# Softplus's last sum on GpSimd, residual sums as adding transfers, the router's last product in token layout, and new beats for a kernel of 16 batches

## The reference

```python
x = x + layernorm(attn(layernorm(x)))     # attn: a selective scan (Mamba block)
x = x + layernorm(ffn(layernorm(x)))      # ffn: two branches of 8 low-rank experts

# attn(x), di = 512 channels, N = 16 states, 4 taps
h = x * rsqrt(mean(x * x) + EPS) * norm_scale
xs, res = split(h @ w_in);  res = silu(res);  xs = silu(causal_conv(xs) + conv_b)
delta, B, C = split(xs @ w_xproj, [16, 32])
delta = softplus(delta @ w_dt + b_dt)
state[t] = exp(delta[t] * A) * state[t-1] + (delta[t] * xs[t]) * B[t]      # per channel and state
y[t] = sum over the 16 states of state[t] * C[t]
return x + ((y + xs * D) * res) @ w_out

# ffn(x), per branch (Q, K, V, W, U differ)
prod = (Q @ V) * cumsum(K @ W)                        # 8 experts of rank 64
weights = softmax(gelu(Q @ router_w1.T + b1) @ router_w2.T + b2 + expert_bias)   # 8 values a token
out = ((prod * weights) @ U + weights @ b) / (t + 1)
return (fwd + 0.5 * inv) @ W_O.T
```

## Time and profile before

| | |
|---|---|
| median of 3 runs | 2423.53 us (2418.75 to 2423.81) |
| the profiled execution | 2417.08 us, of which the span of instructions is 2415.1 us |
| first scan starts, last scan ends | 68.2 and 2294.9 us |
| busy: VectorE, TensorE, GpSimd, ScalarE | 2173.3, 2128.0, 1854.3, 1842.0 us |
| transfers | 101.69 MB, in mean 42 GB/s |

### The profile page before, as it was taken

One profiled execution on the slowest core, in us unless ns is written; L12 is line 12 of the kernel. 1 busy time (PEld: TensorE's weight loads), 2 busy tenths in 40 slices (PEclk: granted clock), 3 DMA queues, 4 the chain that ended last, 5 costly groups with the idle time before them and its releaser, 6 DMA issues.

```text
span 2415.1 us, 35863 instructions
## 1 busy us (share of the span) xinstructions
PE 2128.0 (88%) x9268; PEld 1287.7 (53%) x9268; DVE 2173.3 (90%) x2820; ACT 1842.0 (76%) x3897; POOL 1854.3 (77%) x1324
## 2 busy tenths in 40 slices
PE   5587789898998989899898989989898998988888
PEld 2355455464655546465554645555464655545454
DVE  1899999999999999999999999999998999999921
ACT  6575787869688786978778697887869788785644
POOL 3869797887879788787878878797887879787620
PEclk8797899999999999999999999999999999999999
DMA  6011110211102020111102021110202001011100
GB/s 139 31 40 41 31 49 19 67 31 59 36 28 58 18 71 28 62 32 34 52 20 68 28 62 33 30 55 23 67 27 62 31 29 56 21 60 34 31 2 16
DMA packets 83400, 101.69 MB, mean 42 GB/s; under 512 B 23480, under 2 KB 49872, under 8 KB 83168
## 3 DMA queue, kind: packets, MB, share of 16 engines
q1 hardware_dynamic: 83168, 99.06, 13.6%
HBM read 90.13 MB, written 8.91 MB: 41 GB/s over the span
## 4 chain that ended last, share of the span: by engine, by line
DVE 34%; issue 26%; PE 19%; POOL 11%; ACT 8%; DVEq 1%; DMA 1%; POOLq 0%; ACTq 0%; SPq 0%
DVE h L1347 15%; DVE yT L1363 11%; PE bank L798 10%; POOL bx L766 5%; PE stateT L971 3%; PE bank L950 3%; DVE xs L1257 2%; ACT decay L1217 2%; POOL scratch L684 1%; POOL scratch L690 1%; DVE rows L1283 1%; DVE prod L1329 1%; POOL dx L694 1%; PE bank L936 1%; DVE cumT L1303 1%
## 5 line engine op out<-in xcount | busy, mean ns | idle before, releaser
L766 POOL TENSOR_TENSOR bx<-dx,B_rows 128x1024 f32<-128x1024 f32 x512 | 1204.8, 2366 | 224.3 <-DVE h L1347 183.8
L1347 DVE TENSOR_TENSOR_SCAN h<-decay,bx 128x512 f32<-128x512 f32 x1024 | 1238.6, 1210 | 65.6 <-ACT decay L1217 54.8
L1217 ACT ACTIVATE decay<-delta,decay_rate 128x512 f32<-128x512 f32 x1024 | 703.2, 693 | 273.5 <-DVE h L1347 270.4
L971 PE MATMUL stateT<-ident,h 128*128 128x128 f32 x4096 | 640.7, 288 | 200.7 <-DVE h L1347 107.0
L971 PEld LDWEIGHTS stateT<-ident,h 128*128 128x128 f32 x4096 | 482.6, 146 | 541.1 <-issue 269.1
L1363 DVE SCALAR_TENSOR_TENSOR yT<-stateT,C_tok,yT 128x512 f32<-128x512 f32 x960 | 696.4, 726 | 24.9 <-PE stateT L971 23.8
L798 PE MATMUL bank<-k_to_expert,cumT 128*128 128x512 f32 x512 | 261.2, 635 | 6.8 <-DVE prod L1329 6.7
L798 PE MATMUL bank<-q_to_expert,xnT 128*128 128x512 f32 x512 | 249.2, 611 | 0.0
L798 PE MATMUL bank<-hT,w_in_sb 128*128 128x512 f32 x512 | 243.2, 600 | 5.5 <-DVE rows L1283 3.6
L1183 ACT ACTIVATE cum_sb<-bank,gate 128x64 f32<-128x64 f32 x1024 | 222.7, 328 | 28.7 <-PE bank L798 26.9
L950 PE MATMUL bank<-expert_to_out,prodT 128*128 128x256 f32 x1024 | 239.2, 379 | 0.0
(11 more groups left out here) (155 smaller groups left out, 2578.4 us busy)
## 6 DMA issues: line engine op xcount, KB each, us to landing
B_rows<-B_scratch SPq DMA_DIRECT2D x256, 256.0 KB, 3.2
x_front<-in_L_attn_x SPq DMA_DIRECT2D x16, 512.0 KB, 4.9
x_back<-in_L_attn_x SPq DMA_DIRECT2D x16, 512.0 KB, 4.1
out<-x_back SPq DMA_DIRECT2D x16, 512.0 KB, 4.2
w_in_sb<-in_L_attn_w_in SPq DMA_DIRECT2D x1, 1024.0 KB, 5.9
cum_sb<-in_L_ffn_V_fwd SPq DMA_DIRECT2D x2, 256.0 KB
prod<-in_L_ffn_W_inv_exp SPq DMA_DIRECT2D x2, 256.0 KB
xnT<-in_L_ffn_W_fwd SPq DMA_DIRECT2D x2, 256.0 KB
```

The source lines that it names most:

```text
L766: pool.tensor_tensor(bx[use % BX_RING][:, :, :], dx[q.parity][:, 2 * half:2 * half + 2, :], row, ALU.mult).then_inc(s_bx.step(f"{n},{half} ...
L971: last = pe.transpose(stateT[j % 2][:, c * P:(c + 1) * P], h[n % 2][:, c, j * P:(j + 1) * P], ident[:, :])
L1217: act.activation(decay[c % 2][:, :], delta[q.parity][:, c, :], ACT.Exp, scale=decay_rate[:, c, n:n + 1]).then_inc(s_exp.step(f"{n},{c}"), 1)
L1347: dve.tensor_tensor_scan(h[n % 2][:, c, :], decay[c % 2][:, :], bx[(2 * n + c // 2) % BX_RING][:, c % 2, :], 0.0, ALU.mult, ALU.add).then_ ...
```

## The change

Four edits in one.

1. `d1` moves from VectorE to GpSimd, with the same operation on the same tiles. All that waited for VectorE's d1 (decays, `dx`, reuse of `scratch`) waits for GpSimd's.
2. `x1` and `x` become transfers that GpSimd issues, from `rows` and `o_rows` into `x_back`, both in SBUF, with `accum_op=ALU.add`; `x` is one transfer of all 512 KB instead of two halves. `st1` and the store wait for the transfers' semaphores.
3. `logit` takes blocks of 128 tokens of `scratch` as the stationary operand and 8 columns of weights as the moving one, so that the result has tokens on partitions. ScalarE's copy and `logit_rows` fall away; TensorE has one use of a bank fewer a period. The wait for the batch before's last output product moves from the copy to `gateT`.
4. `TIMETABLE` is new throughout.

```diff
-    ("F", "sq", "act"): (12,),
+    ("F", "sq", "act"): (2,),
-    ("F", "w", "pool"): (102, 103, 119, 124),
-    ("F", "w2", "pool"): (102, 105, 122, 125),
-    ("F", "d1", "dve"): (96, 105, 123, 123),
-    ("F", "row", "sp"): (87, 110, 113),
+    ("F", "w", "pool"): (100, 107, 118, 120),
+    ("F", "w2", "pool"): (103, 111, 120, 125),
+    ("F", "d1", "pool"): (105, 113, 125, 126),
+    ("F", "row", "sp"): (111, 117, 136),
...
-    ("F", "silu", "act"): (70,),
+    ("F", "silu", "act"): (66,),
-    ("B", "rb", "pool"): (301,),
-    ("B", "t", "act"): (299,),
-    ("B", "x1", "pool"): (304,),
-    ("B", "st1", "dve"): (304,),
+    ("B", "rb", "pool"): (305,),
+    ("B", "t", "act"): (303,),
+    ("B", "x1", "pool"): (307,),
+    ("B", "st1", "dve"): (307,),
-    ("B", "xnT", "pe"): (317, 317),
-    ("B", "rt", "pe"): (324, 325, 327, 330),
+    ("B", "xnT", "pe"): (316, 318),
+    ("B", "rt", "pe"): (320, 325, 327, 330),
...
-    ("L", "out", "pe"): (373, 382, 396, 396, 434, 436, 438, 443),
+    ("L", "out", "pe"): (378, 387, 397, 398, 438, 442, 447, 451),
-    ("L", "rs", "pool"): (454,),
-    ("L", "t", "act"): (468,),
-    ("F", "dx", "pool"): (108, 109, 127, 131),
-    ("L", "x", "pool"): (476, 479),
-    ("L", "store", "sp"): (471,),
+    ("L", "rs", "pool"): (464,),
+    ("L", "t", "act"): (469,),
+    ("F", "dx", "pool"): (113, 115, 129, 130),
+    ("L", "x", "pool"): (478,),
+    ("L", "store", "sp"): (463,),
...
             def store(batch, k, use):
-                sp.wait_ge(l_pool.sem, l_pool.done(batch, "x1"))
+                sp.wait_ge(out_added, batch.count(16, 16))
...
+            def d1_task(b, c, use):
+                pool.wait_ge(f_act.sem, f_act.done(b, f"ln{c}"))
+                pool.wait_ge(f_pool.sem, f_pool.done(b, f"w2{c}"))
+                pool.tensor_tensor(delta[b.parity][:, c, :], delta[b.parity][:, c, :], scratch[:, 2 + c % 2, :], ALU.add).then_inc(f_pool.step(f"d1{c}"), 1)
...
             def x_task(b, k, use):
-                half = slice(2 * k, 2 * k + 2)
-                pool.wait_ge(l_act.sem, l_act.done(b, f"t{2 * k + 1}"))
-                pool.tensor_tensor(x_back[b.parity][:, half, :], x_back[b.parity][:, half, :], o_rows[:, half, :], ALU.add).then_inc(l_pool.step(f"x{k}"), 1)
+                pool.wait_ge(l_act.sem, l_act.done(b, "t3"))
+                pool.sem_inc(passed["pool"], 1)
+                pool.dma_start(x_back[b.parity][:, :, :], o_rows[:, :, :], accum_op=ALU.add).then_inc(out_added, 16)
...
             def x1_task(b, k, use):
                 pool.wait_ge(b_act.sem, b_act.done(b, "t3"))
-                pool.tensor_tensor(x_back[b.parity][:, :, :], x_back[b.parity][:, :, :], rows[:, :, :], ALU.add).then_inc(b_pool.step("x1"), 1)
+                pool.sem_inc(passed["pool"], 1)
+                pool.dma_start(x_back[b.parity][:, :, :], rows[:, :, :], accum_op=ALU.add).then_inc(back_added, 16)
...
-                matmuls(use.bank[0:2 * KE, :], [(w2_padded[:, m, (1 - br) * KE:(3 - br) * KE], scratch[:, 2 * br + m, :])
-                                                for br in range(2) for m in range(DT)]).then_inc(b_pe.step("lg"), 1)
+                for j in range(TB):
+                    for br in range(2):
+                        columns = slice((2 * j + br) * KE, (2 * j + br + 1) * KE)
+                        last = matmuls(use.bank[:, columns], [(scratch[:, 2 * br + m, j * P:(j + 1) * P], w2_padded[:, m, KE:2 * KE]) for m in range(DT)])
+                last.then_inc(b_pe.step("lg"), 1)
```

More of the change, by code:

```diff
@@ L144 @@
-    ("B", "logit", "act"): (343,),
-    ("B", "logit_rows", "pe"): (343,),
-    ("B", "lb", "dve"): (342,),
-    ("B", "mx", "dve"): (344,),
-    ("B", "sub", "pool"): (353,),
-    ("B", "ex", "act"): (349,),
+    ("F", "sq", "act"): (2,),
+    ("F", "rs", "pool"): (18,),
+    ("F", "h", "act"): (19,),
+    ("F", "hT", "pe"): (21, 23),
+    ("F", "hT", "act"): (23, 26),
+    ("F", "x", "sp"): (102,),
+    ("F", "xs", "pe"): (32, 34, 36, 38),
+    ("F", "xs", "act"): (35, 36, 38, 42),
+    ("F", "cvA", "dve"): (34, None, 37, None),
@@ new lines @@
+    ("F", "cvB", "dve"): (35, None, 38, None),
+    ("F", "cvC", "dve"): (36, None, 39, None),
+    ("F", "tap", "act"): (None, 38, None, 42),
+    ("F", "cv", "pool"): (None, 45, None, 60),
+    ("F", "res", "pe"): (36, 42, 45, 53),
+    ("F", "res", "act"): (41, 44, 53, 61),
+    ("F", "silu", "act"): (66,),
+    ("F", "proj", "pe"): (79,),
+    ("F", "proj", "act"): (84,),
+    ("F", "B", "sp"): (86,),
+    ("F", "Ct", "pe"): (117,),
+    ("F", "Ct", "act"): (122,),
+    ("F", "dt", "pe"): (85, 87, 93, 103),
@@ new lines @@
+    ("F", "dt", "act"): (87, 94, 104, 108),
+    ("F", "ex", "act"): (90, 94, 106, 115),
+    ("F", "ln", "act"): (90, 99, 112, 117),
+    ("F", "w", "pool"): (100, 107, 118, 120),
+    ("F", "w2", "pool"): (103, 111, 120, 125),
+    ("F", "d1", "pool"): (105, 113, 125, 126),
+    ("F", "row", "sp"): (111, 117, 136),
+    ("B", "y", "pe"): (264, 265, 265, 266),
+    ("B", "u", "dve"): (264, 264, 264, 268),
+    ("B", "o", "pool"): (272, 273, 274, 277),
+    ("B", "wo", "pe"): (278, 280, 283, 287),
@@ new lines @@
+    ("B", "r", "dve"): (282, 282, 289, 290),
+    ("B", "st", "dve"): (291,),
+    ("B", "ag", "dve"): (294,),
+    ("B", "rb", "pool"): (305,),
+    ("B", "t", "act"): (303,),
+    ("B", "x1", "pool"): (307,),
+    ("B", "st1", "dve"): (307,),
+    ("B", "ag1", "dve"): (308,),
+    ("B", "rb1", "pool"): (313,),
+    ("B", "xn", "act"): (314,),
+    ("B", "xnT", "pe"): (316, 318),
+    ("B", "xnT", "act"): (320, 320),
+    ("B", "cum", "dve"): (319, 319),
+    ("B", "rt", "pe"): (320, 325, 327, 330),
@@ L150 @@
+    ("B", "rt", "act"): (327, 330, 332, 332),
+    ("B", "gelu", "act"): (337,),
+    ("B", "logit", "pe"): (340,),
+    ("B", "lb", "dve"): (340,),
+    ("B", "mx", "dve"): (342,),
+    ("B", "sub", "pool"): (351,),
+    ("B", "ex", "act"): (347,),
     ("B", "sm", "dve"): (348,),
[L151 removed]
+    ("B", "sn", "pool"): (357,),
     ("B", "rc", "dve"): (348,),
[L153 to L156 removed]
@@ L157 @@
-    ("L", "xv", "pe"): (349, 359, 367, 378, 394, 423, 426, 431),
-    ("L", "cum", "act"): (356, 358, 369, 378, 390, 392, 408, 433),
[4 rows of a table removed]
-    ("L", "out", "act"): (388, 400, 442, 445),
-    ("L", "sq", "act"): (450,),
-    ("L", "rs", "pool"): (454,),
-    ("L", "t", "act"): (468,),
-    ("F", "dx", "pool"): (108, 109, 127, 131),
-    ("L", "x", "pool"): (476, 479),
-    ("L", "store", "sp"): (471,),
+    ("B", "wa", "pool"): (359,),
+    ("B", "gT", "pe"): (364,),
+    ("B", "gT", "act"): (366,),
@@ L170 @@
+    ("L", "cum", "pe"): (346, 358, 365, 375, 382, 391, 402, 432),
+    ("L", "xv", "pe"): (353, 363, 367, 378, 395, 422, 430, 434),
+    ("L", "cum", "act"): (356, 361, 369, 379, 392, 393, 411, 438),
[4 rows of a table added]
+    ("L", "out", "act"): (388, 400, 446, 455),
+    ("L", "sq", "act"): (456,),
+    ("L", "rs", "pool"): (464,),
[3 more added lines that the diff above has]
+    ("L", "store", "sp"): (463,),
 }
```

105 lines of the change are left out of this document (27 added, 78 removed), and 8 rows, old and new, of tables (FILLED_BY, TIMETABLE).

## The result

The changed kernel takes **2459.7 us** in the median of four runs (2449.7 to 2462.0), the kernel before 2423.4 us beside it: ratio 1.0146, with 95% interval 1.0116 to 1.0177. It is 1.5% slower. The profiled execution has a span of 2457.2 us, 42.1 us more than before.

The account below looks back on a forecast made before the run. VectorE bounds the kernel now; after the change GpSimd binds the stretch from beat 90 to 132. Terms 0.6 + 14.3 - 2 + 0 + 2 + 7.8 = +22.7 on 2417.1: 2440, 2446 as median, given as 2445; range 2404 to 2492 us.

Parts of the forecast that it names:

- GpSimd binds the stretch: From the scan of beat 90 to that of beat 132: 42.3 us against 42.26 now, 15 times, +0.6 us.
- the sign named for them: Profile sign: VectorE's waits for `bx` rise from 10.7 to over 30 us, at beats 0 and 4.
- the new beats: The remaining moves in the timetable (sq, silu, rs, row 2 of B): costed at 0, ends -5 and +5 us.
- The wait for row 13 of B: GpSimd before bx (13,0), behind the store on SyncE: 1.1 us in each of 13 periods, +14.3 us.
- D: Time from an adding transfer's issue to its landing: taken as 6.0 us, with ends 4.2 and 9.
- rival 1: Adding transfers are quick (4.2 us), no wait for row 13: +4.8 us, 2422, as a median 2428; chance 0.2.
- Fewer stalls by TensorE: In the periods, router's product in token layout takes 3.8 us, hidden behind VectorE: -2 us in all (0 to -7).
- the router in the tail: Behind the last scan, the chain loses ScalarE's copy and two waits as well: -2.5 us.
- Head: Ahead of the first scan, the four softplus sums in one chain on GpSimd: +2 us, between +0.8 and +5.1.
- Tail: At the end: x1's transfer +2.6, output products' order +3.3, last residual sum +4.4, router -2.5: +7.8 us.
- Rival 2: VectorE stays the bound of the stretch: -26 us, 2391, as a median 2397; chance 0.13, a part of it 0.08.
- rival 3: Adding transfers are slow (9 us), row 13 and st1 wait each period: about +100 us, 2524 as a median; chance 0.12.

Follow-up runs that it names:

- e3: The kernel before with softplus's last sum (d1) alone moved to GpSimd, at beats 106, 107, 124, 126: 2449.8 us, ratio 1.0109.
- e1: The changed kernel with the old router product back (8 passes of 512 columns, ScalarE's copy, four transposes): 2432.8 us, ratio 1.0040 to the kernel before.
- e9: e1 with softplus's last sum back on VectorE and both residual sums again additions of GpSimd, so the new beats alone: 2492.1 us, ratio 1.0285 to the kernel before.
- e4: The kernel before with only its two residual sums turned into adding transfers issued by GpSimd: 2428.5 us, ratio 1.0022.

## Why the prediction was right, and where it was not

The sign, the range (2404 to 2492) and the order of size were right; 2445 was forecast, 2459.7 came (+22.7 us by the sum, +42.1 between the profiled spans). But two large steps behind the number were wrong, and they offset each other: 14.3 us were forecast for a wait that isn't there, and 31 us came from a clock that the prediction doesn't mention. That the number came out near is luck.

- **GpSimd binds the stretch** (42.3 us forecast, +0.6 in all). Right: 41.92 us, GpSimd busy for 41.30 (42.0 forecast), VectorE for 39.15 (38.8). The 48 us taken from VectorE in 64 sums gave 5.2 in the stretches. VectorE's waits for `bx` came at beats 0 and 4, as foreseen, but the sign named for them failed: they rose from 10.7 to 17.7 us (without the one ahead of the first scan), not to over 30. That the move costs the periods next to nothing holds for the new order alone: e3 shows that the same move in the old one costs 33 us in the periods. That interplay of the parts is not in the prediction; it costed the new beats at 0. With the moved sums they bring the periods back to 0.7 us of before (e1), so they are worth some 33 us there, and without them they cost 74.5 (e9, together with the unmoved additions).
- **The wait for row 13 of B**, D - 4.9 each, +14.3. The formula gives nothing at the measured D of 4.6, and there is no such wait: the changed kernel's GpSimd never waits for rows of B. D was mis-sized at 6.0: the plain transfer's 4.2 us was the nearer end. By the prediction's own signs (no wait for rows of B, landings near 4) this was rival 1. By the page "DMA: Bandwidth & Descriptors", section "Anatomy of one DMA", with the two sources of "Collectives: The Full Stack", section "The bandwidth ceiling", the Trainium skill's estimate had been 4.4 us; the trace agrees to 0.2.
- **Fewer stalls by TensorE**, -2, and **the router in the tail**, -2.5. This step failed. The product's own length was forecast well (3.8 us; 3.64 at the full clock), but it was costed only as time that TensorE spends, and it takes up to 6.8 us in the periods and 7.0 in the tail where the clock is low. What counts is the clock behind it: +25 us in the periods and +6.2 in the tail (changed against e1), 26 us by the ratios.
- **Head**, +2 (ends 0.8 and 5.1): 4.2 in e3, inside the ends; 0.0 in the changed kernel, outside them.
- **Tail**, +7.8: measured 16.3. Of it the transfers are 5.7 (e4; forecast 2.6 + 4.4), the order of the output products and what goes with it 4.4 (e1 less e4; forecast 3.3), the router +6.2 instead of -2.5.

With D = 4.6 the prediction's own terms give 0.6 - 2 + 2 + 5.0 = +5.6 (tail 1.2 + 3.3 + 3.0 - 2.5), 2423 for an execution like the profiled one and 2429 as a median, beside rival 1: it would have missed by 31 us. Rival 1 was right on the transfers and wrong on the time, for the same reason. Rival 2 is excluded (no stretch falls under 41 us in the changed kernel or in e1), and rival 3 as well (landings of 4.6 us; in the periods the statistics of x1 wait once, for 0.4 us).
